# State-space mixer: state sums by accumulating transposes, and four units scanned wholly in PSUM

## The chip, the cores and the metric

The program runs on one core of a Trainium2 chip. The metric is the device time of one execution in microseconds (us), the median of several runs. The engines are TensorE (PE, with its weight loads PEld), VectorE (DVE), ScalarE (ACT), GpSimd (POOL) and SyncE (SP), which here issues all the transfers.

## The reference

A feed-forward block, a mixer and the same feed-forward block again work on x of 4 sequences of 2048 tokens and 512 channels, all in f32. The change is in the mixer alone:

```
xz = x_in @ W_in;  x, z = split(xz)            # 1024 channels each
x  = silu(depthwise_conv4(x) + conv_b)
Bm, Cm = split(x @ W_x)                         # 16 states each
delta  = softplus(x @ W_dt + b_dt)
# for each channel d and state s, over tokens t:
h[d,s] = exp(delta[t,d] * A[d,s]) * h[d,s] + delta[t,d] * Bm[t,s] * x[t,d]
y[t,d] = sum_s h[d,s] * Cm[t,s]
out = ((y + x * D) * silu(z)) @ W_out + residual
```

## The kernel before, in words

The mixer cuts the 8192 tokens into 32 chunks of 256 tokens (the columns of a tile) and the 1024 channels into 8 blocks b of 128 (the partitions). The 16 states of a block are taken as 4 groups g of 4. One **unit** n = 4b+g is one group of one block, so that a chunk is 32 units, and a unit has two **pairs** of states (`half` 0 and 1).

For each unit:

- GpSimd makes `dbu` = delta·x·B for two units at once (`times_b`, L948), into a ring of 4 units.
- ScalarE makes exp(delta·A) of two states into one of three PSUM banks `ps_da` (L1154). First it waits until that bank is free. If the bank held a first pair, it must first copy the last column of the states aside (`keep_psum`, L1095), and for that VectorE's product with C (L1257) must be done.
- VectorE runs four scans (L1245). The first pair is scanned in its PSUM bank; the second pair from PSUM into the SBUF ring `hp`.
- The first pair is multiplied by C on VectorE into `hc` (`times_c`, L1257), the second pair by GpSimd in place in `hp` (L961), for two units at once where it can (in the last block one at a time).
- TensorE adds the products: a matmul with the identity as the stationary operand and 256 columns moving, into the PSUM bank `ps_y` of the block (two banks, taken in turn): L1395 for `hc`, L1405 for `hp`. 20 of a chunk's 64 states in `hp` are not added there but by VectorE (`add_state`, L1224): three in each odd block and two in each even one.
- When a block's sum is complete, VectorE multiplies it by the gate (`gated`, L1231). The skip term x·D was written into `ps_y` beforehand by ScalarE (`skip`, L1016), before the first sum of the block.

Beside this run, for later units or the next chunk: the input product (L1333) and its convolution (ScalarE L1003, then three steps on VectorE, L1211), the gate product (L1344) and its copy (L1023), the delta product (L1362) with ScalarE's abs, relu, exp and log (L1062 to L1071), the product for B and C (L1353), and the output product (L1372). Four times a chunk ScalarE loads the table for silu, runs silu on z and on u, and loads the exp table again (L1183, L1028, L1009, L1188). I call this **the table block**; it stands after the exps of a unit n with n mod 8 = 5.

The order of work is written out by hand. A list such as `YG_AT` gives for each block the unit in whose step an engine does the thing; `due` looks it up, also for the neighbouring chunks. All engines walk through the same 32 steps, and semaphores hold them together.

Of the kernel before, what the change touches and what calls it, by code (L numbers as in the profile page):

```python
# [687 lines left out]
def mixer_phase(nc, hT_pad, xs_in, ahead, w_dt, w_out, w_k, mu_r, mu_k, bc_dram, out):  # L688
# [8 lines left out]
    with ExitStack() as ctx:  # L697
# [297 lines left out]
        def _(act):  # L995
# [143 lines left out]
            def body(i, par, first):  # L1139
                for n in range(NU):  # L1140
# [3 lines left out]
                    for half in range(2):  # L1144
                        p = 2 * n + half
                        if before(p) % 2:
                            bank_scanned(i, p)
                        else:
                            keep_psum(i, p)
                        if before(p) % 2 == 0:  # L1150
                            psum_kept(i, p)
# [46 lines left out]
        def _(dve):  # L1198
# [15 lines left out]
            def added_before(c, b):  # L1214
                return sum(len(a) for a in ADDED) * c + sum(len(a) for a in ADDED[:b])

            def add_state(c, b, k):

                y = y_sum(b)
                if k == 0:  # L1220
                    dve.wait_ge(s_r, NU * c + NG * (b + 1))
                else:
                    dve.wait_ge(s_ya, added_before(c, b) + k)
                V.tensor_tensor(y, y, hp[:, ADDED[b][k] % NH, SG - SD - 1, :], ALU.add).then_inc(s_ya, 1)  # L1224
# [323 lines left out]
```

## Time and profile before

| | us |
|---|---|
| median of 3 runs | 5237.82 (5236.78 to 5240.89) |
| span of the profiled execution | 5236.4 |
| PE busy in the span | 5093.7 (97%) |
| DVE | 4729.5 (90%) |
| POOL | 4028.2 (77%) |
| ACT | 3830.1 (73%) |

The time of the profiled execution is its span; what the runs show beyond it is 1.4 us at the median. The mixer fills the span from about 665 us to 4630 us; before and behind it are the two feed-forward blocks. The busy shares over the whole span mix the three. Two neighbouring instructions of one engine overlap a little in the rows, so what an instruction costs its engine is read from its start to the start of the next, which is less than its duration.

### The profile page before, as it was taken

To read this page: it belongs to the slowest core of one execution; us is meant where nothing else is said; L and a number is where in the kernel's file an instruction comes from. 1 tells how busy PE (TensorE), PEld (TensorE's weight loads), DVE (VectorE), ACT (ScalarE), POOL (GpSimd) and SP (SyncE) were. 2 spreads that over 40 slices of the span, in tenths; PEclk is the share of its full clock that TensorE was granted. 3 is DMA by queue.
4 is the path that set the end of the run, shared out by engine and by line. 5 is a ranking of instruction groups with operands and counts; after the bars stand their busy time and mean duration, and the time that the engine had idled before them with its cause. 6 is when DMAs were issued, how large, how long until landed. Compare 5 with 4: busy or idle time off the path is not lost. (4 is left out here: it accounts for less than half of the span.)

```text
span 5236.4 us, 76648 instructions
## 1 busy us (share of the span) xinstructions
PE 5093.7 (97%) x22144; PEld 4077.0 (78%) x22144; DVE 4729.5 (90%) x8180; ACT 3830.1 (73%) x9592; POOL 4028.2 (77%) x1701
## 2 busy tenths in 40 slices
PE   8999989999999999999999999999999999989999
PEld 6777767777777777777777777777777777768887
DVE  6777679999999999999999999999999999977775
ACT  5566468888888888888888888888888888744443
POOL 1111069999999999999999999999999999931110
PEclk9999999999999999999999999999999999989999
DMA  2222231111111111111111111111111111111111
GB/s 83 96 73 83 99 109 45 45 45 53 57 53 49 45 45 45 45 45 45 50 52 48 46 52 55 53 54 45 45 45 45 45 45 45 65 53 57 65 57 41
DMA packets 137370, 291.71 MB, mean 56 GB/s; under 512 B 23280, under 2 KB 40688, under 8 KB 136944
## 3 DMA queue, kind: packets, MB, share of 16 engines
q1 hardware_dynamic: 136944, 286.75, 16.5%
q8 instruction: 180, 2.95, 0.2%
q14 instruction: 246, 2.02, 0.1%
HBM read 218.53 MB, written 68.18 MB: 55 GB/s over the span
## 5 line engine op out<-in xcount | busy, mean ns | idle before, releaser
L948 POOL TENSOR_TENSOR mx_dbu<-mx_bs,mx_du 128x2048 f32<-128x2048 f32 (+1 forms) x513 | 2326.9, 4536 | 60.0 <-DVE mx_hp L1245 49.8
L1154 ACT ACTIVATE mx_ps_da<-mx_dl,mx_a 128x256 f32<-128x256 f32 x4096 | 1775.8, 465 | 53.8 <-DVE mx_hp L1245 19.0
L1245 DVE TENSOR_TENSOR_SCAN mx_hp<-mx_ps_da,mx_hst,mx_dbu 128x256 f32<-128x256 f32 x1792 | 1313.9, 733 | 30.9 <-ACT mx_ps_da L1154 30.9
L1245 DVE TENSOR_TENSOR_SCAN mx_ps_da<-mx_ps_da,mx_hst,mx_dbu 128x256 f32<-128x256 f32 x1792 | 1248.8, 736 | 21.6 <-ACT mx_ps_da L1154 15.7
L961 POOL TENSOR_TENSOR mx_hp<-mx_hp,mx_cs 128x1024 f32<-128x1024 f32 (+1 forms) x576 | 1224.7, 2133 | 1.7 <-ACT mx_hst L1077 1.7
L1395 PE MATMUL mx_ps_y<-mx_hc,mx_ident 128*128 128x256 f32 x4096 | 1054.7, 380 | 2.0 <-ACT mx_ps_y L1016 2.0
L1362 PE MATMUL mx_ps_m<-mx_u,mx_w_dt 128*128 128x256 f32 x4096 | 927.7, 380 | 2.3 <-issue 2.3
L1395 PEld LDWEIGHTS mx_ps_y<-mx_hc,mx_ident 128*128 128x128 f32 x4096 | 779.9, 190 | 109.8 <-ACT mx_ps_y L1016 2.8
L1362 PEld LDWEIGHTS mx_ps_m<-mx_u,mx_w_dt 128*128 128x128 f32 x4096 | 779.2, 190 | 109.4 <-issue 3.1
L1405 PE MATMUL mx_ps_y<-mx_hp,mx_ident 128*128 128x256 f32 x2816 | 787.3, 383 | 50.6 <-POOL mx_hp L961 50.5
L1405 PEld LDWEIGHTS mx_ps_y<-mx_hp,mx_ident 128*128 128x128 f32 x2816 | 525.6, 190 | 233.3 <-issue 87.9
L1257 DVE TENSOR_TENSOR mx_hc<-mx_ps_da,mx_cs 128x512 f32<-128x512 f32 x1024 | 682.1, 666 | 4.1 <-issue 2.1
L1095 ACT ACTIVATE mx_hst<-mx_ps_da 128x2 f32<-128x2 f32 x1022 | 171.2, 168 | 632.6 <-DVE mx_hc L1257 631.6
L246 POOL TENSOR_TENSOR f_rstd<-f_ve,f_half 128x4 f32<-128x4 f32 x48 | 48.4, 1009 | 681.3 <-DVE f_ve L413 681.3
L1344 PE MATMUL mx_ps_m<-mx_hT,mx_w_in 128*128 128x256 f32 x2048 | 493.8, 383 | 24.8 <-DVE mx_u L1211 23.8
L1333 PE MATMUL mx_ps_m<-mx_hT,mx_w_in 128*128 128x259 f32 x2048 | 492.2, 383 | 5.1 <-PEq L59 3.2
L1333 PEld LDWEIGHTS mx_ps_m<-mx_hT,mx_w_in 128*128 128x128 f32 x2048 | 389.4, 190 | 104.7 <-issue 46.4
L1372 PE MATMUL mx_ps_c<-mx_w_out,mx_gy 128*128 128x512 f32 x992 | 467.2, 593 | 0.0
L1344 PEld LDWEIGHTS mx_ps_m<-mx_hT,mx_w_in 128*128 128x128 f32 x2048 | 381.0, 190 | 108.0 <-DVE mx_u L1211 56.0
L1211 DVE SCALAR_TENSOR_TENSOR mx_u<-mx_ps_m,mx_cw,mx_u 128x256 f32<-128x256 f32 x768 | 354.9, 462 | 28.6 <-ACT mx_u L1003 27.8
L252 POOL TENSOR_TENSOR mx_w_in<-f_xhT 128x2048 f32<-128x2048 f32 x30 | 112.1, 3738 | 324.2 <-ACT f_xhT L302 324.2
L1372 PEld LDWEIGHTS mx_ps_c<-mx_w_out,mx_gy 128*128 128x128 f32 x992 | 189.1, 191 | 132.1 <-issue 119.2
(122 smaller groups left out, 7378.5 us busy)
## 6 DMA issues: line engine op xcount, KB each, us to landing
mx_bs<-bc_scratch SPq DMA_DIRECT2D x128, 512.0 KB, 4.6
mx_cs<-bc_scratch SPq DMA_DIRECT2D x128, 512.0 KB, 3.8
mx_hT<-hT_scratch SPq DMA_DIRECT2D x32, 518.0 KB, 4.2
hT_scratch<-f_h2T SPq DMA_DIRECT2D x16, 1024.0 KB, 9.1
mx_xo<-xs_scratch SPq DMA_DIRECT2D x32, 512.0 KB, 3.6
x_scratch<-mx_xo SPq DMA_DIRECT2D x32, 512.0 KB, 2.9
f_x<-in_L_attn_inp SPq DMA_DIRECT2D x12, 1024.0 KB, 6.6
xs_scratch<-f_x SPq DMA_DIRECT2D x12, 1024.0 KB, 4.3
```

The lines of the kernel that those rows point to most:

```text
L948: G.tensor_tensor(dbu[:, n % NM:n % NM + k].rearrange("p n s t -> p (n s) t"), bs[:, g:g + k].rearrange("p n s t -> p (n s) t"), bcast(du[ ...
L961: G.tensor_tensor(h, h, cs[:, g:g + k, SD:SG, :], ALU.mult).then_inc(s_pr, k)
L1154: ins = A.activation(ps_da[DA_BANK[p]][:, k, :], dl[:, b % NL, :], ACT.Exp, scale=a_sb[:, b, s:s + 1])
L1211: V.scalar_tensor_tensor(out=q, in0=in_bank(b)[:, step:step + T], scalar=cw[:, step, b:b + 1], in1=q, op0=ALU.mult, op1=ALU.add).then_inc( ...
L1245: ins = V.tensor_tensor_scan(da if half == 0 else hp[:, n % NH, k, :], da, dbu[:, n % NM, s, :], 0.0 if first else hst[:, b, SG * g + s:SG ...
L1257: V.tensor_tensor(hc[:, n % NC, :, :], ps_da[DA_BANK[2 * n]][:, :, :], cs[:, g, 0:SD, :], ALU.mult).then_inc(s_m2, 1)
L1333: ins = M.matmul(in_bank(b)[:, 0:TH], w_in_sb[:, f, b * P:(b + 1) * P], hT[cp][:, f, :], start=(f == 0), stop=(f == NB - 1))
L1344: ins = M.matmul(m_bank(b)[:, 0:T], w_in_sb[:, f, DI + b * P:DI + (b + 1) * P], hT[cp][:, f, PAD_L:PAD_L + T], start=(f == 0), stop=(f == ...
L1362: ins = M.matmul(m_bank(b)[:, 0:T], w_dt_sb[:, k, b * P:(b + 1) * P], u[:, cp, k, :], start=(k == 0), stop=(k == ND - 1))
L1372: ins = M.matmul(ps_c[:, :], gy[:, cp, b, j * P:(j + 1) * P], w_out_sb[:, b, :], start=False, stop=(b == ND - 1), skip_group_check=True)
L1395: ins = M.matmul(y_sum(b), ident[:, :], hc[:, n % NC, k, :], start=False, stop=False, skip_group_check=True)
L1405: ins = M.matmul(y_sum(b), ident[:, :], hp[:, n % NH, k, :], start=False, stop=(g == NG - 1), skip_group_check=True)
```

## The change

- **The sum.** The matmul with the identity is gone. Each product with C is now turned: the data is the stationary operand, the identity moves, and the transpose accumulates in `ps_y` (`turn_onto`). `ps_y` holds tokens in the partitions and channels in the columns. A state of 256 tokens takes two transposes of 128 columns. All states are summed so; `add_state` on VectorE is gone, with its 20 instructions a chunk.
- **Back.** When a block is complete, ScalarE copies it to the new tile `yt` (`copy_y`), then writes the skip term into `ps_y` (`skip`, which stood at step 4b+3, ahead of the block's first sum, and now stands at step 4b+9, behind its last), and TensorE turns `yt` back onto it with two transposes (`turn_back`). The gate product on VectorE (`gated`) moves from step 4b+9 to step 4b+10.
- **Units 4, 5, 20 and 21.** Their second pair is scanned in PSUM too, and VectorE multiplies it by C into the new tile `hx` (`times_c_second`), one unit later, behind the next unit's first scan. GpSimd's product for these units (two instructions a chunk) is gone. ScalarE keeps the state of these pairs from PSUM (`keep_psum` for them too).

```diff
-        SKIP_AT = [NG * b + NG - 1 for b in range(ND)]
-        ADDED = [[n for n in range(NG * b + 1 + (b % 2 == 0), NG * (b + 1))] for b in range(ND)]
-        YG_AT = [NG * b + NG + 5 for b in range(ND)]
+        YT_AT = [NG * b + NG + 5 for b in range(ND)]
+        BACK_AT = [NG * b + NG + 5 for b in range(ND)]
+        YG_AT = [NG * b + NG + 6 for b in range(ND)]
+        ALL_IN_PSUM = (4, 5, 20, 21)
...
+            def copy_y(c, b):
+                act.wait_ge(s_r, NU * c + NG * (b + 1))
+                A.activation(yt[:, b % 2, :], y_sum(b), ACT.Copy).then_inc(s_yt, 1)
+
             def skip(c, cp, b):
                 act.wait_ge(s_u, ND * c + 2 * (b // 2) + 2)
-                if not (is0(c) and b < 2):
-                    act.wait_ge(s_g, ND * c + (b - 1))
+                act.wait_ge(s_yt, ND * c + (b + 1))
                 A.activation(y_sum(b), u[:, cp, b, :], ACT.Copy, scale=d_sb[:, b:b + 1]).then_inc(s_yd, 1)
...
                     scan(i, n, 0, 0, first)
-                    add_due(i, n, 0)
+                    if n - 1 in ALL_IN_PSUM:
+                        times_c_second(i, n - 1)
                     scan(i, n, 0, 1, first)
-                    add_due(i, n, 1)
...
+            def times_c_second(i, n):
+                g, e = n % NG, extra(n)
+                dve.wait_ge(s_sc, 2 * NU * i + (2 * n + 2))
+                if not (is0(i) and e < NX2):
+                    dve.wait_ge(s_rcx, NE * i + (e - NX2 + 1))
+                V.tensor_tensor(hx[:, e % NX2, :, :], ps_da[DA_BANK[2 * n + 1]][:, :, :], cs[:, g, SD:SG, :],
+                                ALU.mult).then_inc(s_m2x, 1)
...
+            def turn_onto(b, pair, first):
+                for k in range(SD):
+                    for j in range(TJ):
+                        ins = M.matmul(y_sum(b)[:, j * P:(j + 1) * P], pair[:, k, j * P:(j + 1) * P], ident[:, :],
+                                       is_transpose=True, start=(first and k == 0 and j == 0), stop=False,
+                                       skip_group_check=True)
+                return ins
...
             def sum_psum_states(c, n):
                 b, g = divmod(n, NG)
-                if g == 0:
-                    pe.wait_ge(s_yd, ND * c + (b + 1))
+                if g == 0 and not (is0(c) and b < 2):
+                    pe.wait_ge(s_g, ND * c + (b - 1))
                 pe.wait_ge(s_m2, NU * c + (n + 1))
-                for k in range(SD):
-                    ins = M.matmul(y_sum(b), ident[:, :], hc[:, n % NC, k, :],
-                                   start=False, stop=False, skip_group_check=True)
-                ins.then_inc(s_rc, 1)
+                turn_onto(b, hc[:, n % NC], g == 0).then_inc(s_rc, 1)
...
+            def turn_back(c, b):
+                pe.wait_ge(s_yd, ND * c + (b + 1))
+                for j in range(TJ):
+                    ins = M.matmul(y_sum(b)[:, j * P:(j + 1) * P], yt[:, b % 2, j * P:(j + 1) * P], ident[:, :],
+                                   is_transpose=True, start=False, stop=(j == TJ - 1), skip_group_check=True)
+                ins.then_inc(s_yb, 1)
```

The program also asks for a smaller scratch for transfers that GpSimd would issue (`dynamic_dma_scratch_size=1024`); no transfer in either kernel is issued by GpSimd.

**VectorE in a table block's steps, before.** These are the rows of steps 5 and 6 (mod 8) of a chunk's middle, from the last convolution step of step 4. L1245 is a scan (into `ps_da` for the first pair, into `hp` for the second), L1257 the product with C, L1224 an added state, L1231 the gate.

```order
L1211 SCALAR_TENSOR_TENSOR mx_u<-mx_ps_m,mx_cw,mx_u 128x256
L1245 SCALAR_TENSOR_TENSOR mx_ps_da<-mx_ps_da,mx_hst,mx_dbu 128x256
L1224 TENSOR_TENSOR mx_ps_y<-mx_ps_y,mx_hp 128x256
L1245 SCALAR_TENSOR_TENSOR mx_ps_da<-mx_ps_da,mx_hst,mx_dbu 128x256
L1224 TENSOR_TENSOR mx_ps_y<-mx_ps_y,mx_hp 128x256
L1245 SCALAR_TENSOR_TENSOR mx_hp<-mx_ps_da,mx_hst,mx_dbu 128x256
L1257 TENSOR_TENSOR mx_hc<-mx_ps_da,mx_cs 128x512
L1224 TENSOR_TENSOR mx_ps_y<-mx_ps_y,mx_hp 128x256
L1245 SCALAR_TENSOR_TENSOR mx_hp<-mx_ps_da,mx_hst,mx_dbu 128x256
L1231 TENSOR_TENSOR mx_gy<-mx_ps_y,mx_gy 128x256
```

The same steps in the changed kernel, where lines 1253, 1275, 1288 and 1261 stand for 1211, 1245, 1257 and 1231:

```order
L1253 SCALAR_TENSOR_TENSOR mx_u<-mx_ps_m,mx_cw,mx_u 128x256
L1275 SCALAR_TENSOR_TENSOR mx_ps_da<-mx_ps_da,mx_hst,mx_dbu 128x256 x2
L1275 SCALAR_TENSOR_TENSOR mx_hp<-mx_ps_da,mx_hst,mx_dbu 128x256
L1288 TENSOR_TENSOR mx_hc<-mx_ps_da,mx_cs 128x512
L1275 SCALAR_TENSOR_TENSOR mx_hp<-mx_ps_da,mx_hst,mx_dbu 128x256
L1275 SCALAR_TENSOR_TENSOR mx_ps_da<-mx_ps_da,mx_hst,mx_dbu 128x256 x2
L1275 SCALAR_TENSOR_TENSOR mx_hp<-mx_ps_da,mx_hst,mx_dbu 128x256
L1288 TENSOR_TENSOR mx_hc<-mx_ps_da,mx_cs 128x512
L1275 SCALAR_TENSOR_TENSOR mx_hp<-mx_ps_da,mx_hst,mx_dbu 128x256
L1261 TENSOR_TENSOR mx_gy<-mx_ps_y,mx_gy 128x256
```

The three added states are gone from step 5, and the gate stands one step later, at the end of step 6.

**ScalarE around a table block, before.** L1095 and L1077 keep states, L1154 are the exps of a pair, L1183 and L1188 the two table loads with silu of z and u between, L1062 and L1063 abs and relu, L1023 the gate product's copy, L1067 the exp of the softplus, L1016 the skip term.

```order
L1077 ACTIVATE mx_hst<-mx_hp 128x2
L1154 ACTIVATE mx_ps_da<-mx_dl,mx_a 128x256 x2
L1095 ACTIVATE mx_hst<-mx_ps_da 128x2
L1154 ACTIVATE mx_ps_da<-mx_dl,mx_a 128x256 x2
L1077 ACTIVATE mx_hst<-mx_hp 128x2
L1183 ACT_TABLE_LOAD
L1028 ACTIVATE mx_gy<-mx_gy 128x512
L1009 ACTIVATE mx_u<-mx_u 128x512
L1188 ACT_TABLE_LOAD
L1154 ACTIVATE mx_ps_da<-mx_dl,mx_a 128x256 x2
L1062 ACTIVATE mx_en<-mx_ps_m,mx_bdt 128x256
```

The same in the changed kernel (1116, 1192, 1136, 1222, 1065, 1042, 1227 and 1099 stand for 1077, 1154, 1095, 1183, 1028, 1009, 1188 and 1062; L1047 is `copy_y`, L1053 `skip`):

```order
L1116 ACTIVATE mx_hst<-mx_hp 128x2
L1192 ACTIVATE mx_ps_da<-mx_dl,mx_a 128x256 x2
L1047 ACTIVATE mx_yt<-mx_ps_y 128x256
L1053 ACTIVATE mx_ps_y<-mx_u,mx_d 128x256
L1136 ACTIVATE mx_hst<-mx_ps_da 128x2
L1192 ACTIVATE mx_ps_da<-mx_dl,mx_a 128x256 x2
L1116 ACTIVATE mx_hst<-mx_hp 128x2
L1222 ACT_TABLE_LOAD
L1065 ACTIVATE mx_gy<-mx_gy 128x512
L1042 ACTIVATE mx_u<-mx_u 128x512
L1227 ACT_TABLE_LOAD
L1192 ACTIVATE mx_ps_da<-mx_dl,mx_a 128x256 x2
```

The copy and the skip term now stand just before the exps that lead into the table block; from that block on the order is as it was.

**TensorE from a delta product over a gate product, before** (L1362 the delta product, L1344 the gate product, L1353 the product for B and C):

```order
L1362 MATMUL mx_ps_m<-mx_u,mx_w_dt 128x256 x8
L1405 MATMUL mx_ps_y<-mx_hp,mx_ident 128x256 x2
L1395 MATMUL mx_ps_y<-mx_hc,mx_ident 128x256 x2
L1344 MATMUL mx_ps_m<-mx_hT,mx_w_in 128x256 x4
L1405 MATMUL mx_ps_y<-mx_hp,mx_ident 128x256 x2
L1395 MATMUL mx_ps_y<-mx_hc,mx_ident 128x256 x2
L1353 MATMUL mx_ps_c<-mx_u,mx_w_x 32x256 x8
```

and in the changed kernel (1395, 1377 and 1386 stand for 1362, 1344 and 1353; L1425 is `turn_onto`, L1453 `turn_back`):

```order
L1395 MATMUL mx_ps_m<-mx_u,mx_w_dt 128x256 x8
L1425 MATMUL mx_ps_y<-mx_ident,mx_hp 128x128 x4
L1425 MATMUL mx_ps_y<-mx_ident,mx_hc 128x128 x4
L1377 MATMUL mx_ps_m<-mx_hT,mx_w_in 128x256 x4
L1425 MATMUL mx_ps_y<-mx_ident,mx_hp 128x128 x4
L1425 MATMUL mx_ps_y<-mx_ident,mx_hc 128x128 x4
L1453 MATMUL mx_ps_y<-mx_ident,mx_yt 128x128 x2
L1386 MATMUL mx_ps_c<-mx_u,mx_w_x 32x256 x8
```

Two or one wide matmuls become four narrow transposes, and two more stand behind the gate product's step.

## Rows read from the trace of the kernel before

**Rows 1.** Windows; stretch, length, busy (count) PE PEld DVE ACT POOL, clock, DMA.

```profile
2000.00:3000.00 1000.00, 987.15 (x4248) 790.68 (x4247) 978.41 (x1730) 815.36 (x2206) 983.24 (x408) 1.00 0.15 49
...
4480.00:4600.00 120.00, 107.59 (x423) 81.81 (x422) 113.53 (x191) 91.32 (x253) 120.00 (x51) 0.96 0.19 62
```

**Rows 2.** Instructions of one tile, 1880:2045; count, ns, first to last start.

```profile
L1055 ACT ACTIVATE mx_bc<-mx_ps_c x2: 357/357/357, 1900.8 to 2023.1; 32x256 f32<-32x256 f32 x2
```

**Rows 3.** Timeline, VectorE, a table block's steps; start, duration, engine, line.

```profile
2017.33 0.75 DVE L1245 TENSOR_TENSOR_SCAN mx_hp<-mx_ps_da,mx_hst,mx_dbu 128x256 f32<-128x256 f32 x1 [0.33 <-ACT mx_ps_da L1154]
...
2039.53 0.67 DVE L1257 TENSOR_TENSOR mx_hc<-mx_ps_da,mx_cs 128x512 f32<-128x512 f32 x1
...
2042.21 0.40 DVE L1224 TENSOR_TENSOR mx_ps_y<-mx_ps_y,mx_hp 128x256 f32<-128x256 f32 x1
2042.52 0.74 DVE L1245 TENSOR_TENSOR_SCAN mx_ps_da<-mx_ps_da,mx_hst,mx_dbu 128x256 f32<-128x256 f32 x1
...
2045.72 0.39 DVE L1231 TENSOR_TENSOR mx_gy<-mx_ps_y,mx_gy 128x256 f32<-128x256 f32 x1
2046.17 1.40 DVE L1245 TENSOR_TENSOR_SCAN mx_ps_da<-mx_ps_da,mx_hst,mx_dbu 128x256 f32<-128x256 f32 x2
2047.90 0.75 DVE L1245 TENSOR_TENSOR_SCAN mx_hp<-mx_ps_da,mx_hst,mx_dbu 128x256 f32<-128x256 f32 x1 [0.33 <-ACT mx_ps_da L1154]
```

**Rows 4.** Timeline, ScalarE, the same table block.

```profile
2040.24 0.17 ACT L1095 ACTIVATE mx_hst<-mx_ps_da 128x2 f32<-128x2 f32 x1 [1.59 <-DVE mx_hc L1257]
...
2045.27 0.87 ACT L1154 ACTIVATE mx_ps_da<-mx_dl,mx_a 128x256 f32<-128x256 f32 x2
...
2046.99 0.87 ACT L1154 ACTIVATE mx_ps_da<-mx_dl,mx_a 128x256 f32<-128x256 f32 x2
...
2047.90 0.36 ACT L1023 ACTIVATE mx_gy<-mx_ps_m 128x256 f32<-128x256 f32 x1
...
2049.27 0.46 ACT L1016 ACTIVATE mx_ps_y<-mx_u,mx_d 128x256 f32<-128x256 f32 x1
...
2055.98 0.17 ACT L1095 ACTIVATE mx_hst<-mx_ps_da 128x2 f32<-128x2 f32 x1 [0.93 <-DVE mx_hc L1257]
```

**Rows 5.** Timeline, TensorE, identity sums between delta and gate product.

```profile
2040.36 1.03 PE L1405 MATMUL mx_ps_y<-mx_hp,mx_ident 128*128 128x256 f32 x4
2041.22 1.03 PE L1395 MATMUL mx_ps_y<-mx_hc,mx_ident 128*128 128x256 f32 x4
2042.08 1.89 PE L1344 MATMUL mx_ps_m<-mx_hT,mx_w_in 128*128 128x256 f32 x8
```

**Rows 6.** Timeline, TensorE, eight transposes in the first feed-forward block.

```profile
321.48 1.09 PE L566 MATMUL f_ps_t<-f_ident,f_h 128*128 128x128 f32 x8
322.32 0.48 PE L601 MATMUL f_ps_kr<-f_w_lo,f_xr_hi 128*128 128x512 f32 x1
322.64 0.41 PE L602 MATMUL f_ps_kr<-f_w_hi,f_xr_hi 128*128 128x512 f32 x1
```

**Rows 7.** Timeline, GpSimd: its product with C for two units.

```profile
2035.26 2.37 POOL L961 TENSOR_TENSOR mx_hp<-mx_hp,mx_cs 128x1024 f32<-128x1024 f32 x1
```

**Rows 8.** Windows as rows 1: around the fall of TensorE's clock near 2668 us.

```profile
2664.71:2668.12 3.41, 1.29 (x6) 1.17 (x7) 1.88 (x4) 2.34 (x8) 3.41 (x4) 1.00 0.40 133
2668.12:2671.54 3.42, 3.42 (x10) 2.67 (x9) 3.42 (x8) 2.34 (x9) 3.42 (x1) 0.50 0.61 180
```

**Rows 9.** Timeline, TensorE: delta products in and outside that stretch.

```profile
2036.90 3.62 PE L1362 MATMUL mx_ps_m<-mx_u,mx_w_dt 128*128 128x256 f32 x16
...
2666.82 5.40 PE L1362 MATMUL mx_ps_m<-mx_u,mx_w_dt 128*128 128x256 f32 x16 [2.32 <-issue]
```

**Rows 10.** Windows, the transposes (tile f_ps_t) alone: PE busy, clock, DMA.

```profile
4641.03:4644.44 3.41, 3.41 (x17) 0.50 0.96 350
4644.44:4647.86 3.42, 1.06 (x8) 1.00 0.00 1
```

More of the change, by code:

```diff
@@ L41 @@
 NC = 4
+NX2 = 2
 NH = 8
@@ L799, in mixer_phase, with in_psum, extra, step_to @@
         DA_BANK = [p % NA for p in range(2 * NU - 1)] + [1]
+        ALL_IN_PSUM = (4, 5, 20, 21)
+        NE = len(ALL_IN_PSUM)
+        def in_psum(p):
+            return p % 2 == 0 or p % (2 * NU) // 2 in ALL_IN_PSUM
+        def extra(n):
+            return sum(m < n for m in ALL_IN_PSUM)
+        def step_to(n):
+            k = 1
+            while n - k in ALL_IN_PSUM:
+                k += 1
+            return k
+        def last_in_sbuf(n):
+            while n % NU in ALL_IN_PSUM:
+                n -= 1
+            return n
         def is0(i):
@@ L1145, in body @@
                         p = 2 * n + half
-                        if before(p) % 2:
+                        if in_psum(before(p)):
+                            keep_psum(i, p)
+                        else:
                             bank_scanned(i, p)
[L1148 to L1151, printed above, removed]
                         for k in range(SD):
@@ L1160, in body @@
                                 first_tap(i + s, (par + s) % 2, bb)
-                            for bb, s in due(SKIP_AT, n, i):
+                            for bb, s in due(YT_AT, n, i):
+                                copy_y(i + s, bb)
                                 skip(i + s, (par + s) % 2, bb)
@@ L1193, in epilogue @@
                         keep(LAST, NU + n - KEEP_LAG)
+                    for b in due_after(YT_AT, n):
+                        copy_y(LAST, b)
+                        skip(LAST, LAST % 2, b)
             over_chunks(act, prologue, body, epilogue)
@@ L1212, in conv @@
                                        in1=q, op0=ALU.mult, op1=ALU.add).then_inc(s_cq if step == KC - 1 else s_cv, 1)
[L1214 to L1224, printed above, removed]
             def gated(c, cp, b):
@@ L1309, in epilogue @@
                     for b in due_after(YG_AT, n):
-                        for k in range(len(ADDED[b])):
-                            add_state(LAST, b, k)
                         gated(LAST, LAST % 2, b)
@@ L1453, in body @@
                         sum_psum_states(i - 1, NU + n - SUMC_LAG)
+                    for b, s in due(BACK_AT, n, i):
+                        turn_back(i + s, b)
             def epilogue():
-                for n in range(SUM_LAG):
+                for n in range(BACK_AT[-1] + 1 - NU):
+                    if n < SUM_LAG:
+                        sum_states(LAST, NU + n - SUM_LAG)
+                    if n < SUMC_LAG:
+                        sum_psum_states(LAST, NU + n - SUMC_LAG)
+                    for b in due_after(BACK_AT, n):
+                        turn_back(LAST, b)
                     if n == 2:
```

73 lines of the change are left out of this document (41 added, 32 removed).

## The prediction

> **What bounds the kernel now.** I read the busy time in windows first. In the mixer's steady part three engines look full at once: TensorE 987, GpSimd 983 and VectorE 978 us of 1000; ScalarE has 815 [rows 1]. A share alone doesn't say which of the three sets the pace, so I looked for a chain that closes on itself. One chunk lasts 122.3 us (the copy of B and C, once a chunk, starts at 1900.8 and 2023.1) [rows 2], and a chunk has four table blocks, so eight steps last 30.6 us.
>
> The timeline of VectorE around a table block shows the chain. I cut the eight steps at two places: the product with C of step 4 (mod 8) and the third scan of step 6.
>
> - Stretch A, from the product at 2039.53 to the scan at 2047.90, is 8.37 us [rows 3]. ScalarE runs it. The product ends, ScalarE keeps the state at 2040.24, makes two exps, loads the table, runs silu twice, loads the table back, makes the exps at 2045.27, abs and relu, and the exps at 2046.99; the scan starts 0.04 us after these end [rows 4]. VectorE waits twice in it: two scans that start at 2046.17 would have let the third start 1.30 us later (1.40 less the usual overlap of 0.1), at 2047.47, so 0.43 are lost there, and about 0.14 between the gate at 2045.72 (0.31 long, start to start) and 2046.17. VectorE's own work in A is thus 7.8 us.
> - Stretch B, from such a scan at 2017.33 to the product at 2039.53, is 22.20 us [rows 3], VectorE without a gap.
>
> A and B give 30.57, four times 122.3: the chunk exactly. TensorE and GpSimd are nearly full, but the chain that closes is VectorE and ScalarE. That is the reading on which the forecast rests: **what VectorE saves in B counts, what it saves in A becomes a longer wait for ScalarE.**
>
> **VectorE.** An added state costs 0.31 (2042.21 to 2042.52) [rows 3], 0.32 as a mean. Of the 20 of a chunk, 12 (three in each odd block) stand in step 5, in A, and 8 (two in each even block) in step 1, in B. The gates leave steps 1 and 5 and come to steps 2 and 6, both in B. So B loses two states and a gate and gains two gates: 22.20 − 0.64 + 0.31 = 21.87. A's own work falls by three states and a gate, 1.27, to 6.5, far below 8.37: A stays as it is and the wait grows from 0.6 to 1.8 us.
>
> The second product of units 4, 5, 20 and 21 costs 0.67 less the overlap of 0.09, 0.58 [rows 3]. For both pairs of units it stands in A (steps 5 and 6), where there is room. Only its order shows: the exps at 2045.27 are ready at 2046.14, 6.6 us into A, and then a scan (0.65), the product (0.58) and a scan (0.65) come before the third scan, 8.52 instead of 8.37. A scan into PSUM costs what one into SBUF does, since both are 0.65 apart in B's steps.
>
> **ScalarE.** It gains a copy of 256 columns from PSUM in each block, 0.36 as the gate product's [rows 4], and a semaphore wait on itself before the skip term of 0.46; together some 0.8 us in step 1 (mod 4), between its two exps. There it waits now for the product with C: 1.59 us before the table block [rows 4], 0.93 in the tightest such step that I found [rows 4]. So it is hidden, with 0.1 us to spare there. The skip term leaves step 3, where ScalarE was just catching up behind the table block. Keeping the second pairs from PSUM (0.17) replaces keeping them from SBUF in the four units. Bounds of this edit: nothing, and the whole 0.8 us in each of 8 steps, 6.4 us a chunk, if no wait covered it.
>
> **TensorE.** A chunk has 64 + 44 = 108 identity matmuls. Four records, two matmuls, take 0.86 (2040.36, 2041.22, 2042.08) [rows 5], so 46.4 us go. 256 transposes and 16 turned back come. Eight take 0.84 (321.48 to 322.32) and the first matmul after them is 0.32 from the next where 0.23 is usual [rows 6], so 0.105 each and some 0.14 for each of the 32 groups of eight: 28.6 + 4.5 = 33.1 us. TensorE falls from 120.7 us a chunk (98.7%) [rows 1] to about 107. These transposes write and don't add; one that accumulates isn't shown. From above I bound it by the transposes at the lower clock, 17 in 3.41 us, 0.20 each [rows 10]; that would be +26 us, 133 in all. TensorE would set the pace from 0.155 each on. I take 0.105, the row that is nearest: same shape, same clock.
>
> What queues behind the new waits: TensorE's `turn_back` in step 4b+9 waits for ScalarE's skip term of the same step. In front of it stand the gate product (from 2042.08, 1.73 long) and eight transposes, while ScalarE's exps of that step ended before 2040.24; so it is there in time. The first sum of block b+2 in step 4b+11 now waits for VectorE's gate at the end of step 4b+10; behind it stand the delta products, needed only by relu two steps later. TensorE will idle some 1 us there and 2.5 us before the gate product, whose convolution ends only with step 0 (mod 4). That is idle time of an engine with 14 us a chunk to spare.
>
> **GpSimd.** Two products with C of 2.37 [rows 7] leave each chunk: 4.7 us of about 120. It isn't in the chain, except in the last chunk, where no input products are left and GpSimd is busy 120.00 of 120.00 us from 4480 to 4600 [rows 1]. There I count 3.5 us. The end of the mixer: three added states become copy, skip term and two transposes, about 1.3 us each way, nothing.
>
> **The sum.** Per chunk four times (−0.64 + 0.31), and twice +0.15: −1.0 us. 31 chunks: −31; the last: −3.5. Together −34.5 on the profiled execution's 5236.4, so 5202. The runs' median is 1.4 above that execution: 5203.
>
> At the clock I weigh a rule. Transposes alone filled the stretch from 4641.03 to 4644.44 at the granted clock 0.50, and it was 1.00 in the next [rows 10]: TensorE did nothing but transposes and rose to 2.4 GHz. The Trainium skill, TensorE: Matmul & The Clock Gate, Part 4 (PE-mode transpose), says that in transpose mode the full clock doesn't engage, because a transpose isn't counted as activity. By this rule a quarter of TensorE's work would turn into apparent idleness and the mixer could sink to 1.2 GHz; here the trace disagrees.
>
> **The rivals.**
>
> 1. *All of VectorE's saving arrives* (the table block isn't the limit). 20 × 0.32 − 4 × 0.58 = 4.1 us a chunk, 5237.8 − 131 = 5107. For it: GpSimd (about 115.5 us then) and TensorE (107) would allow it, and 815 of 1000 us leaves ScalarE room on average. Against: the scan at 2047.90 starts 0.04 us after its exps, with the added states still in A.
> 2. *TensorE's clock falls in its new idle stretches* (slower). Between 2664.71 and 2668.12 TensorE was busy 1.29 of 3.41 us, and the next 3.4 us ran at 0.50 [rows 8]; the delta product at 2666.82 took 5.40 us where 3.62 is usual [rows 9], 1.8 us lost. My idle stretch of 2.5 us before a gate product is as long as the 2.32 there. Eight falls a chunk add 14 us: 121.4 against a chunk of 121.3. It decides where four steps are full already. They hold 107 / 8 = 13.4 us of 15.2 on average, and some 1.3 more in two of the eight: where the product for B and C stands (eight matmuls, about 3.5 as the delta product, and no output product) and where two output products do. A fall makes each of these 14.7 + 1.8 = 16.5, late by 1.3, and a chunk lasts 121.3 + 2.6 = 123.9: +1.5 a chunk, 5237.8 + 48 = 5286. For it: the idle stretches are real. Against: a late TensorE waits less before the next gate product, so falls thin themselves out.
> 3. *ScalarE's 0.8 us doesn't fit* in step 1 (mod 4): if the wait between copy and skip term costs 0.25 more than I think, 0.12 us in each of eight steps eat the gain: 5237.
> 4. *The clock sinks throughout* by the rule above: TensorE twice 107 us a chunk, +92 × 32: 8170.
>
> **How the numbers follow.** A change within 0.2%, 10.5 us, can't be told from none here. Forecast 0.53, its own range 5190 to 5222, all faster. Rival 1 0.12, faster. Rival 2 0.19, slower but for mild cases. Rival 3 0.13, split over no change and its two sides. Rival 4 0.03. Faster 0.64, same 0.14, slower 0.22. For the range I leave out rivals 1 and 4 and half a tenth beyond rival 2: 5140 to 5290; the low end takes in the part of rival 1 in which A shortens somewhat.
>
> **What would show it.** In the profile after: the distance of two copies of B and C 121.3 us; the third scan of step 6 waiting for ScalarE's exps by 1.3 to 1.8 us four times a chunk, in all some 1.6 × 4 × 32 = 200 us of VectorE's idle time before its scans, released by ScalarE's exps; the table block itself unchanged; transposes 0.105 us apart; TensorE's busy share near 90%, GpSimd's near 95%. The forecast is wrong if A is shorter than 8.3 us, if the delta or input products wait for anything but their old partners, if TensorE's clock in the mixer's windows is below 0.97 and ScalarE waits for its products, or if VectorE shows no new wait.

## The result, and the profile after

The changed kernel takes 5295.2 us (median of 4 runs, 5294.0 to 5296.5), the kernel before 5239.4: 1.0108 times as long, 95% interval 1.0093 to 1.0122. The forecast was 5203. It had the wrong sign, and the time lies 5 us above its range of 5140 to 5290.

In the profiled executions (5236.4 and 5292.2) the copy of B and C cuts the span into its start, 31 chunks and the end. Tile view of that copy, before and then after; count, ns, first to last start:

```profile
L1055 ACT ACTIVATE mx_bc<-mx_ps_c x32: 357/357/373, 692.1 to 4471.8; 32x256 f32<-32x256 f32 x32
```

```profile
L1092 ACT ACTIVATE mx_bc<-mx_ps_c x32: 357/357/374, 692.0 to 4532.7; 32x256 f32<-32x256 f32 x32
```

The start is the same. The 31 chunks take 3779.7 before and 3840.7 after, +61.0; the rest 764.6 and 759.5, −5.1. Together, but for 0.1 at the start, +55.8: all of the loss lies in the chunks. They take 123.9 us on average, 121.9 before; the forecast's cut of 1.0 would have made it 120.9. The averages hold the first chunk and those at a change of sequence (every eighth), which are shorter. A chunk in a sequence's middle takes 122.5 or 122.6 before and 124.1 to 125.8 after. Windows of after (columns as rows 1); the second begins and ends with a copy of B and C, the last three lie around the loss:

```profile
2000.00:3000.00 1000.00, 879.51 (x4629) 701.94 (x4628) 926.92 (x1572) 828.06 (x2232) 930.13 (x387) 0.96 0.15 48
...
1916.00:2041.20 125.20, 110.84 (x577) 88.49 (x576) 116.46 (x197) 103.03 (x279) 115.78 (x49) 0.95 0.15 47
...
1967.97:1971.38 3.41, 1.09 (x8) 0.86 (x8) 2.63 (x6) 3.35 (x11) 3.41 (x2) 1.00 0.00 0
1971.38:1974.79 3.41, 1.78 (x2) 0.84 (x3) 3.41 (x7) 2.88 (x9) 2.24 (x2) 0.51 0.01 2
1974.79:1978.21 3.42, 3.42 (x7) 2.01 (x6) 2.64 (x5) 0.00 (x0) 1.93 (x1) 0.50 0.00 0
```

Against [rows 1] no engine is full any more, and the granted clock is 0.96 and not 1.00. The longest waits of after between 1000 and 4500 us (total, times, longest) say who waits. The first and the last weren't in the forecast:

```profile
ACT mx_u L1036 <- PE mx_ps_m L1366: 166.0, 59, 5.6
DVE mx_ps_da L1275 <- ACT mx_ps_da L1192: 138.3, 114, 1.7
...
DVE mx_hp L1275 <- ACT mx_ps_da L1192: 106.0, 85, 4.0
...
PE mx_ps_c L1405 <- DVE mx_gy L1261: 86.7, 28, 3.5
```

28 times in 28 chunks an output product waits for a gate. The timelines of one such chunk (1916.00 to 2041.20) show what hangs on it. TensorE first:

```profile
1968.96 0.60 PE L1425 MATMUL mx_ps_y<-mx_ident,mx_hc 128*128 128x128 f32 x4
1973.01 3.78 PE L1405 MATMUL mx_ps_c<-mx_w_out,mx_gy 128*128 128x512 f32 x4 [3.45 <-DVE mx_gy L1261]
1976.59 2.74 PE L1366 MATMUL mx_ps_m<-mx_hT,mx_w_in 128*128 128x259 f32 x8
```

ScalarE, the exps before its wait and the first tap after it:

```profile
1973.44 0.86 ACT L1192 ACTIVATE mx_ps_da<-mx_dl,mx_a 128x256 f32<-128x256 f32 x2
1979.36 0.56 ACT L1036 ACTIVATE mx_u<-mx_ps_m,mx_cb,mx_cw 128x256 f32<-128x256 f32 x1 [5.07 <-PE mx_ps_m L1366]
```

VectorE over the whole chunk: the products with C of step 4 (L1288), the third scans of step 6, and the gate and the stall between:

```profile
1931.85 0.68 DVE L1288 TENSOR_TENSOR mx_hc<-mx_ps_da,mx_cs 128x512 f32<-128x512 f32 x1
...
1938.50 1.40 DVE L1275 TENSOR_TENSOR_SCAN mx_ps_da<-mx_ps_da,mx_hst,mx_dbu 128x256 f32<-128x256 f32 x2 [1.37 <-ACT mx_ps_da L1192]
1940.22 0.75 DVE L1275 TENSOR_TENSOR_SCAN mx_hp<-mx_ps_da,mx_hst,mx_dbu 128x256 f32<-128x256 f32 x1 [0.33 <-ACT mx_ps_da L1192]
...
1962.09 0.68 DVE L1288 TENSOR_TENSOR mx_hc<-mx_ps_da,mx_cs 128x512 f32<-128x512 f32 x1
...
1970.68 0.72 DVE L1275 TENSOR_TENSOR_SCAN mx_hp<-mx_ps_da,mx_hst,mx_dbu 128x256 f32<-128x256 f32 x1
...
1972.56 0.39 DVE L1261 TENSOR_TENSOR mx_gy<-mx_ps_y,mx_gy 128x256 f32<-128x256 f32 x1
...
1980.93 0.75 DVE L1275 TENSOR_TENSOR_SCAN mx_hp<-mx_ps_da,mx_hst,mx_dbu 128x256 f32<-128x256 f32 x1 [3.50 <-ACT mx_ps_da L1192]
...
1996.13 0.68 DVE L1288 TENSOR_TENSOR mx_hc<-mx_ps_da,mx_cs 128x512 f32<-128x512 f32 x1
...
2004.51 0.75 DVE L1275 TENSOR_TENSOR_SCAN mx_hp<-mx_ps_da,mx_hst,mx_dbu 128x256 f32<-128x256 f32 x1 [0.33 <-ACT mx_ps_da L1192]
...
2026.38 0.68 DVE L1288 TENSOR_TENSOR mx_hc<-mx_ps_da,mx_cs 128x512 f32<-128x512 f32 x1
...
2035.26 0.72 DVE L1275 TENSOR_TENSOR_SCAN mx_hp<-mx_ps_da,mx_hst,mx_dbu 128x256 f32<-128x256 f32 x1
```

Read in order: the output product of blocks 6 and 7 stands in step 7 of the next chunk and needs the gate of block 7, which the change moved from the end of step 5 to the end of step 6. TensorE had its sums done near 1969.5; the gate ends at 1972.95. Meanwhile the clock goes to the lower of its levels (0.51, 0.50: 1.2 GHz), so the output product takes 3.78 us and not 1.88, and the input product behind it 2.74 and not 1.92. The first tap waits 5.07 us for it, and no exps are made meanwhile; VectorE's scan waits 3.50 us for those.

| stretch | before | forecast | after |
|---|---|---|---|
| A, no extra unit | 8.37 | 8.37 | 8.37, 8.38 |
| A of units 4 and 5, scanned in PSUM after | 8.37 | 8.52 | 8.59 |
| A of units 20 and 21, scanned in PSUM after | 8.64 | 8.52 | 8.88 |
| B | 22.20 | 21.87 | 21.87, 21.87 |
| B with step 7 | 22.20 | 21.87 | 25.45 |

The stretches B without step 7 and A without extra units came out as forecast, and A with them is 0.07 and 0.36 longer. The stretch with step 7 has 3.58 us too much: 3.50 of it is that one wait.

The stretch A of units 20 and 21 was already 8.64 in the kernel before, which the forecast had missed. It runs there from the product below to the scan at 2017.33 [rows 3], and ScalarE has one instruction more in it, ahead of the table block (L1048, which clears the bank for B and C):

```profile
2008.69 0.68 DVE L1257 TENSOR_TENSOR mx_hc<-mx_ps_da,mx_cs 128x512 f32<-128x512 f32 x1
```

```profile
2010.56 0.36 ACT L1048 ACTIVATE mx_ps_c<-mx_w_x 32x256 f32<-32x256 f32 x1
```

So the extra units lengthen either stretch A by the same amount, 0.22 and 0.24, where 0.15 was forecast.

### The profile page after: what moved, and what is told of

The parts are those of the page before. It is cut to its first block and busy times, and to the rows that moved or that the text cites. A ratio compares the mean times of both kernels' runs of the same rounds, so it can differ in the third digit from the quotient of the medians.

```text
span 5292.2 us, 79790 instructions
## 1 busy us (share of the span) xinstructions
PE 4723.0 (89%) x23936; PEld 3774.3 (71%) x23936; DVE 4592.8 (87%) x7668; ACT 3937.5 (74%) x9848; POOL 3879.9 (73%) x1637
## 5 line engine op out<-in xcount | busy, mean ns | idle before, releaser
L1275 DVE TENSOR_TENSOR_SCAN mx_ps_da<-mx_ps_da,mx_hst,mx_dbu 128x256 f32<-128x256 f32 x2016 | 1404.8, 736 | 134.7 <-ACT mx_ps_da L1192 133.1
L1275 DVE TENSOR_TENSOR_SCAN mx_hp<-mx_ps_da,mx_hst,mx_dbu 128x256 f32<-128x256 f32 x1568 | 1145.6, 731 | 101.1 <-ACT mx_ps_da L1192 101.1
L994 POOL TENSOR_TENSOR mx_hp<-mx_hp,mx_cs 128x1024 f32<-128x1024 f32 (+1 forms) x512 | 1070.9, 2099 | 1.7 <-ACT mx_hst L1116 1.7
L1377 PE MATMUL mx_ps_m<-mx_hT,mx_w_in 128*128 128x256 f32 x2048 | 541.9, 410 | 309.0 <-DVE mx_u L1253 309.0
L1288 DVE TENSOR_TENSOR mx_hc<-mx_ps_da,mx_cs 128x512 f32<-128x512 f32 x1024 | 681.9, 666 | 2.3 <-PE mx_ps_y L1425 2.2
L1425 PE MATMUL mx_ps_y<-mx_ident,mx_hc 128*128 128x128 f32 x4096 | 629.6, 277 | 22.8 <-DVE mx_gy L1261 22.7
L1425 PEld LDWEIGHTS mx_ps_y<-mx_ident,mx_hp 128*128 128x128 f32 x3584 | 447.1, 143 | 259.4 <-POOL mx_hp L994 116.9
L1425 PE MATMUL mx_ps_y<-mx_ident,mx_hp 128*128 128x128 f32 x3584 | 552.6, 278 | 79.6 <-POOL mx_hp L994 79.4
L1405 PE MATMUL mx_ps_c<-mx_w_out,mx_gy 128*128 128x512 f32 x992 | 523.6, 654 | 93.4 <-DVE mx_gy L1261 93.4
L1366 PE MATMUL mx_ps_m<-mx_hT,mx_w_in 128*128 128x259 f32 x2048 | 511.1, 393 | 5.3 <-PEq L60 3.2
L1425 PEld LDWEIGHTS mx_ps_y<-mx_ident,mx_hc 128*128 128x128 f32 x4096 | 490.3, 144 | 30.7 <-DVE mx_gy L1261 16.2
L1366 PEld LDWEIGHTS mx_ps_m<-mx_hT,mx_w_in 128*128 128x128 f32 x2048 | 394.8, 199 | 116.4 <-issue 61.0
```

The source lines that it names most:

```text
L1275: ins = V.tensor_tensor_scan(da if in_psum(p) else hp[:, n % NH, k, :], da, dbu[:, n % NM, s, :], 0.0 if first else hst[:, b, SG * g + s:S ...
L1288: V.tensor_tensor(hc[:, n % NC, :, :], ps_da[DA_BANK[2 * n]][:, :, :], cs[:, g, 0:SD, :], ALU.mult).then_inc(s_m2, 1)
L1366: ins = M.matmul(in_bank(b)[:, 0:TH], w_in_sb[:, f, b * P:(b + 1) * P], hT[cp][:, f, :], start=(f == 0), stop=(f == NB - 1))
L1377: ins = M.matmul(m_bank(b)[:, 0:T], w_in_sb[:, f, DI + b * P:DI + (b + 1) * P], hT[cp][:, f, PAD_L:PAD_L + T], start=(f == 0), stop=(f == ...
L1405: ins = M.matmul(ps_c[:, :], gy[:, cp, b, j * P:(j + 1) * P], w_out_sb[:, b, :], start=False, stop=(b == ND - 1), skip_group_check=True)
L1425: ins = M.matmul(y_sum(b)[:, j * P:(j + 1) * P], pair[:, k, j * P:(j + 1) * P], ident[:, :], is_transpose=True, start=(first and k == 0 an ...
```

## The experiments

Theory 1: the chunk loses its 3 us in step 7, by the output product's wait for gate 7 and the clock's fall in it. Rivals: the clock's falls at the other new idle places (forecast's rival 2), or ScalarE's new copy and skip term.

**The wait removed from either end, and the idle time filled.** Three kernels from the changed one:

```diff
-OUT_AT = [NU - 6, NU - 2, NU + 2, NU + 7, ...
+OUT_AT = [NU - 6, NU - 2, NU + 2, NU + 8, ...
```

> The changed kernel, with the one output product that waits for the gate of block 7 issued in TensorE's step 8 of the next chunk, not in step 7, so that the input product of step 7 no longer stands behind that wait. Theory (the missed wait): after the change this output product waits 3.45 us for the gate that was moved from step 37 to step 38, TensorE's clock falls meanwhile, and the input product, ScalarE's first tap (5.07 us) and VectorE's scan (3.50 us in some 20 chunks, 2.3 in the others) come late one after the other. Then the chunk loses these waits: 5295 - 20x3.5... less what other waits take over, 5220 (5210 to 5232). Rival (the clock falls at all the new idle places and costs there): the other falls stay, less than half comes back, 5260 or more. Rival (ScalarE's copy and skip, and its block of table loads): nothing of theirs is touched, 5290 or more.

```diff
-YG_AT = [NG * b + NG + 6 for b in range(ND)]
+YG_AT = [NG * b + NG + (5 if b == ND - 1 else 6) for b in range(ND)]
```

> The changed kernel, with VectorE's gate of block 7 alone back at the end of step 37 of 32 (step 5 of the next chunk), where it stood before; the other seven gates stay a step later. The output product keeps its place in step 7. Theory (the missed wait): same gain by the other end of the same wait, 5220 (5210 to 5232), if the turn back is done by then (it ended at 1967.3 in the changed trace, VectorE's step 5 at 1970.0). Rival (clock falls everywhere): 5260 or more. Rival (ScalarE's work): 5290 or more. If gate 7 has to wait for the turn back, VectorE waits instead and the time lies between.

```diff
 j, k = divmod(part, OUT_PARTS)
+if part == 3:
+    for b, s2 in due(IN_AT, n, i):
+        pe.wait_ge(s_rl, ND * (i + s2 - 1) + b)
+        for m in range(2 * NB):
+            M.matmul(in_bank(b)[:, 0:TH], ...)
```

> The changed kernel, with TensorE kept busy in the once-per-chunk wait: ahead of the output product in step 7, 16 products of the input product's shape (3.5 us at full clock) into the bank that the input product then overwrites. The wait for gate 7 stays; only the idle time goes, and with it the fall of the clock. Theory that the clock carries most of the loss: the output product takes 1.9 us and not 3.8, the input product 1.8 and not 2.7, the first tap comes 2.8 us earlier, VectorE's 3.5 us wait shrinks to 0.7: 5225 to 5240. Theory that the wait for the gate alone carries it: 5285 to 5300, or more, since the filler also ends some tenths after the gate.

Measured against the kernel before (5238.4; 5239.8 and 5239.7 beside the later runs): output product later 5198.5, 0.9924 (0.9907 to 0.9940); gate 7 back 5188.0, 0.9904 (0.9887 to 0.9920); filler 5236.6, 0.9997 (0.9988 to 1.0007). Removing the wait gives back 97 and 107 us, more than the 75 expected; both times lie below the expected 5210 to 5232. I had counted the full stall of VectorE in 20 chunks only and added little for the others. In the trace of the changed kernel VectorE waits at this place in each of 30 chunks, 2.3 to 4.0 us, in all 96.2 us, nearly the whole of the 96.7. The wait is the longer the more of the output and the input product falls into the stretch at the lower clock. Windows of the kernel with gate 7 back, two whole chunks:

```profile
2126.40:2247.70 121.30, 108.29 (x578) 87.15 (x577) 116.37 (x197) 103.15 (x279) 115.78 (x49) 0.97 0.15 49
...
3216.40:3337.70 121.30, 105.45 (x577) 84.78 (x577) 116.37 (x197) 103.24 (x280) 115.83 (x49) 1.00 0.15 49
```

Both last 121.3 us, one at a mean clock of 0.97 and one at 1.00. So the falls that are left (most of them in the idle time before gate products) cost nothing here, and that rival falls. The other rival, ScalarE's copy and skip term, falls too: nothing of theirs was touched, and the loss is gone.

The filler keeps the wait for the gate and takes the idle time. Its TensorE, L1489 the filler, and then its VectorE:

```profile
1956.71 3.78 PE L1489 MATMUL mx_ps_m<-mx_hT,mx_w_in 128*128 128x259 f32 x16
1960.33 1.88 PE L1405 MATMUL mx_ps_c<-mx_w_out,mx_gy 128*128 128x512 f32 x4
1962.04 1.92 PE L1366 MATMUL mx_ps_m<-mx_hT,mx_w_in 128*128 128x259 f32 x8
```

```profile
1959.73 0.40 DVE L1261 TENSOR_TENSOR mx_gy<-mx_ps_y,mx_gy 128x256 f32<-128x256 f32 x1
...
1965.56 0.75 DVE L1275 TENSOR_TENSOR_SCAN mx_hp<-mx_ps_da,mx_hst,mx_dbu 128x256 f32<-128x256 f32 x1 [0.97 <-ACT mx_ps_da L1192]
```

With 16 products more, whose results are thrown away, the kernel is 58.6 us faster than the changed one: the output product takes 1.88 again, and VectorE's wait falls from 3.50 to 0.97. Against the kernel with the output product later (the same gates), the loss of 96.7 us splits into 58.6 for the clock and 38.1 for the rest. The 38.1 holds the late gate itself and some 4 us of the filler's own, an estimate (30 chunks of 0.14): the output product starts 0.20 us after the gate's end here (1960.13 to 1960.33), and 0.06 in the changed kernel (1972.95 to 1973.01). The clock's share is thus 58.6 us or a little more.

**All gates back in step 4b+9,** and then also the gate product moved to the end of TensorE's step, behind the sums and the turn back:

```diff
-YG_AT = [NG * b + NG + 6 for b in range(ND)]
+YG_AT = [NG * b + NG + 5 for b in range(ND)]
```

> The changed kernel, with all eight gates at the end of VectorE's step 4b+9, as before the change. Theory (the missed wait): as for gate 7 alone, 5220, and the 0.78 us waits of the first PSUM sums for a gate go too, which stand beside other work and give nothing: within 6 us of the kernel that moves gate 7 alone. Rival: the turn back of a block comes after a gate product that itself waits for VectorE (2.44 us idle, then 1.9 to 3.0 us of products), so VectorE waits for it at the end of step 4b+9: 0.3 to 1 us in 7 of 8 blocks, 70 to 250 us in all, and the kernel is at or over 5290.

```diff
-for b, s in due(GATE_AT, n, i):
-    gate_product(i + s, (par + s) % 2, b)
 ...
 for b, s in due(BACK_AT, n, i):
     turn_back(i + s, b)
+for b, s in due(GATE_AT, n, i):
+    gate_product(i + s, (par + s) % 2, b)
```

> All eight gates at the end of VectorE's step 4b+9, as in the kernel of 5238.0, and in TensorE's steps 1 mod 4 the gate product is issued behind the sums and the turn back, not ahead of them. Theory (the extra 50 us of that kernel were VectorE's wait for a turn back that stood behind a waiting gate product): that wait goes, every second gate now lies in VectorE's idle time before step 6 mod 8 (4 x 0.31 us a chunk), and it beats the kernel with gate 7 alone put back: 5150 to 5185. Rival (the 50 us came from having the gates in step 4b+9 at all, or the gate product now comes too late behind the sums): 5200 or more.

All gates back: 5238.0, 0.9998 (0.9988 to 1.0007), 50 us worse than gate 7 alone, where within 6 us was expected. The rival named the right wait, but too large: it had 70 to 250 us and a time of 5290 or more. TensorE and VectorE at one such gate:

```profile
2054.62 3.53 PE L1377 MATMUL mx_ps_m<-mx_hT,mx_w_in 128*128 128x256 f32 x8 [3.11 <-DVE mx_u L1253]
...
2059.01 0.38 PE L1453 MATMUL mx_ps_y<-mx_ident,mx_yt 128*128 128x128 f32 x2
```

```profile
2059.50 0.42 DVE L1261 TENSOR_TENSOR mx_gy<-mx_ps_y,mx_gy 128x256 f32<-128x256 f32 x1 [1.75 <-PE mx_ps_y L1453]
```

The gate product waits 3.11 us and then runs at half speed (3.53, not 1.9); the turn back stands behind it, and VectorE waits 1.75 us for that, 60.7 us in 3500 (46 waits). Here, and not in the changed kernel, a slow gate product reaches VectorE.

With the gate product last: 5163.2, 0.9855 (0.9839 to 0.9872), the fastest kernel that computes everything, 76 us under the kernel before and 132 under the changed one. Its chunks in the middle of a sequence take 120.3 us. The two orders also test the forecast's cut into A and B. With the output product later, all eight gates lie in B: 121.7 us. With gate 7 back, seven: 121.3. With the gate product last, four: 120.3. So 0.4 for the first gate that goes into A, and 1.0 for three more; a gate costs 0.31 by the prediction's reading.

**What stretch A waits for.** From the kernel with gate 7 back: ScalarE's block without its table loads, and Silu of u and z a plain copy (this leaves part of the computation out):

```diff
-A.preload_act_table_set("silu_and_others")
-A.preload_act_table_set("natural_log_exp_and_others")
-A.activation(q, q, ACT.Silu)
+A.activation(q, q, ACT.Copy)
```

> The kernel with gate 7 alone put back, and ScalarE's block of two table loads made short: it leaves out the table loads, and Silu of u and of z is a plain copy. Theory (stretch A is set by that block): VectorE's 5.3 us of waits a chunk for ScalarE's exponentials go, and VectorE (116.0) and GpSimd (115.8) are left as bounds: chunk 117 to 118.5, 5188 - 31 x 2.8 to 4.3 = 5055 to 5100. Rival (those waits are another chain's, GpSimd's or TensorE's, seen last at ScalarE): 5170 or more.

5060.1, 0.9654 (0.9638 to 0.9670), as expected. Windows:

```profile
2000.00:3000.00 1000.00, 914.11 (x4919) 734.43 (x4918) 983.01 (x1674) 794.09 (x2306) 987.50 (x410) 0.98 0.15 49
```

VectorE (983) and GpSimd (988) fill up at once, and most chunks last 116.2 to 117.6 us. Stretch A without extra units falls from 8.37 to 6.49 us (2039.41 to 2045.90 in this trace), which is VectorE's own work in it: the prediction had 6.5. The block is what stretch A waits for.

Then, from the fastest kernel, the block half a step later (it goes from the end of the step before):

```diff
+block = due(Z_SILU_AT, n, i, 1)
+if half == 0 and block:
+    ...            # table load, silu_z, silu_u, table load
+if half == (1 if block else 0):
     ...            # relu, as before
```

> The fastest kernel so far (5163.2; gates in step 4b+9, gate product last), with ScalarE's block of table load, Silu of z, Silu of u and table load moved by half a step: from the end of step 5 mod 8 to behind the first pair's exponentials of step 6 mod 8; the Abs and Relu of that step follow the second pair's exponentials. Theory (stretch A lasts from the product that frees a PSUM bank to the third scan, with the block ahead of both pairs' exponentials): the first pair of step 6 no longer waits for the block, VectorE's waits there fall from 1.05 + 0.33 to some 0.6: 0.5 to 1 us in each of four stretches, 5163 - 31 x 2 to 4 = 5040 to 5100. Rival (the bank of the first pair is free no earlier, so ScalarE waits for it ahead of the block and all shifts back): 5150 to 5180. Rival (the Silu of u comes later, and x_proj, its DMAs or the later Relu set the time): 5180 or more.

5217.0, 0.9956 (0.9939 to 0.9972): 54 us slower, a miss. ScalarE ahead of the block, and VectorE behind it:

```profile
2980.57 0.17 ACT L1140 ACTIVATE mx_hst<-mx_ps_da 128x2 f32<-128x2 f32 x1 [1.29 <-DVE mx_hx L1299]
...
2981.67 1.28 ACT L1196 ACT_TABLE_LOAD   x1
```

```profile
2986.53 0.75 DVE L1277 TENSOR_TENSOR_SCAN mx_hp<-mx_ps_da,mx_hst,mx_dbu 128x256 f32<-128x256 f32 x1 [1.22 <-ACT mx_ps_da L1192]
```

In the stretches with extra units the bank of step 6's first pair holds unit 4's second pair and is free only after its product with C: ScalarE waits 1.29 us for it ahead of the block, and these stretches A grow from 8.60 and 8.89 to 9.36. That is the first rival's wait, for these. In the other two stretches the gain is there, 7.63 for 8.38. Over a chunk the four stretches A are thus no longer than before; what is lost is lost in B. In the chunk from 2064.4 its four stretches take 22.10, 21.84, 22.49 and 21.84, where 21.51 to 21.53 was the rule, and in each of them VectorE waits once or twice more for exps, by 0.20 to 0.42 us. What holds these exps up there, the record leaves open.

**What the units in PSUM are worth.** None of them, from the kernel with gate 7 back (`ALL_IN_PSUM = ()`); eight, and two, from the fastest kernel (`(4, 5, 12, 13, 20, 21, 28, 29)` and `(4, 5)`):

> The kernel with gate 7 alone put back (5188.0), and no unit whose second pair is scanned in PSUM: the turned sums are all that is left of the change. VectorE loses four products a chunk (4 x 0.6 us), GpSimd gets four back (4 x 1.28 us: 115.8 busy in a chunk of 121.3 becomes some 121). Theory that VectorE and ScalarE's table blocks set the chunk: VectorE had waited for ScalarE where those four products stand, so their going gives nothing, and GpSimd just fits: 5185 to 5195. Rival that GpSimd sets it without them: 121.3 becomes 122.3 or more, 5215 to 5240.

> The kernel before this one in the list (gates in step 4b+9, gate product last), with four more units a chunk scanned in PSUM: 12, 13, 28, 29, the same steps of the blocks that had none. GpSimd loses 4 x 1.28 us a chunk, VectorE gains 4 x 0.6 us, two of them in each stretch where it waits 1.69 us for ScalarE's table block. Theory (VectorE and that block set the chunk): within 8 us of the kernel with four units. Rival (GpSimd's 95% busy still sets the pace outside that stretch): 20 to 60 us faster. Rival (PSUM banks come free later, so ScalarE's exponentials come later too, and the table block with them): 20 us slower or more.

> The same fastest kernel (5163.2) with two units a chunk scanned in PSUM (4 and 5) and not four. Theory (VectorE's work outside the wait for the table block sets the chunk, and GpSimd, 115.9 us busy in a chunk of 120.4 and now 118.4, still fits): 5155 to 5166. Rival (GpSimd's turns set it, and each pair of products that it is spared counts): 5175 to 5200. With four, two and none of the units (none: 5191.2, with the gates elsewhere) this tells what that half of the change is worth.

None: 5191.2, 0.9906 (0.9889 to 0.9923), beside 5188.0 with four. Windows:

```profile
2000.00:3000.00 1000.00, 881.35 (x4772) 706.79 (x4771) 937.22 (x1586) 850.89 (x2298) 994.05 (x413) 0.99 0.15 49
```

GpSimd is at 994 of 1000, just inside. The stretches A are 8.38 and, for units 20 and 21, 8.65, as in the kernel before, so their growth with four units is the units'. Two: 5166.9, 0.9861 (0.9844 to 0.9877), 4 us from four. Eight: 5209.0, 0.9942 (0.9925 to 0.9958), 46 us slower than four, where I expected no difference; chunks of 122.2 instead of 120.3. Two more stretches A grow from 8.38 to 8.60, 0.44 us a chunk. The rest lies in the stretch B that leads into the next chunk, 22.6 to 23.1 where the others take 21.5: there a new wait appears, once a chunk (VectorE's waits, 1000 to 4500 us):

```profile
DVE mx_hc L1288 <- DMA mx_cs<-bc_scratch: 20.2, 15, 1.8
DVE mx_hc L1288 <- issue: 17.2, 13, 2.4
```

15 of the 28 are put down to the transfer of the next chunk's C (`mx_cs`); for the other 13 the profile names no cause. Neither rival named it (the second, 20 us slower or more, is right in size alone), and why the transfer comes late is open. So four units, two or none make a difference of 3 to 4 us, under 0.1%, which can't be told from nothing here; the gain of the two fast kernels comes from the other half of the change, the transposes with the gates' places. In the middle of a sequence the kernel with no unit even has the shorter chunk, 120.9 for 121.3.

## Why the prediction was wrong

- **The step that failed** is "What queues behind the new waits". It followed the moved gate to one waiter, the first sum of block b+2, and said that behind it stand the delta products, with two steps to spare. It missed the second waiter, which thus stood in the sum at nothing: the output product of blocks 6 and 7, two steps after the old place of gate 7 and one after the new one, with the input product, the tap and the exps behind it. It costs 96.7 us (5295.2 to 5198.5 with that product a step later), 58.6 of them by the clock's fall. Without that wait the kernel takes 5198.5, or 5188.0 with gate 7 back in A; the forecast was 5203. That product waits for the gate by its last block's number, so it would have been found by listing every wait on the gates' semaphore. One of the prediction's own signs of being wrong came true: the clock below 0.97 while ScalarE waits for TensorE's products (166.0 us, first tap).
- **How good the rest was** is partly luck. "The chunk exactly" was chance: 122.3 is the distance of two copies early in a sequence, where the chunks in its middle take 122.5 or 122.6, since one stretch A in four is 8.64. From there the forecast's −1.0 would be 121.5 or 121.6, and the kernel with the output product later has 121.6 to 121.9. In the total that is more than made up by the three chunks at a change of sequence, which are 4.0 to 4.9 us shorter than before, and the first two, some 2 us each; the forecast had 1.0 for these too.
- **Stretch B, 21.87:** right to the hundredth. **Stretch A:** right where no unit was added; with units 0.07 and 0.36 over the forecast (8.59, 8.88), 0.27 of the larger because that stretch was 8.64 before. **VectorE's new waits** of 1.3 to 1.8 us for the exps are there in the stretches without extra units: 1.37 + 0.33.
- **ScalarE's copy and skip term** cost nothing: A without extra units and B came out at the 8.37 and 21.87 that were summed without them. That ended rival 3.
- **Transposes:** 0.44 us for four, 0.11 each, where 0.105 was taken. With gate 7 back TensorE has 105.5 us a chunk at full clock, 107 forecast. Timeline of after; at 2000.12 and 2000.56 four transposes that accumulate, and behind them the two that turn back:

```profile
2000.12 0.60 PE L1425 MATMUL mx_ps_y<-mx_ident,mx_hp 128*128 128x128 f32 x4
2000.56 0.60 PE L1425 MATMUL mx_ps_y<-mx_ident,mx_hc 128*128 128x128 f32 x4
2001.00 0.38 PE L1453 MATMUL mx_ps_y<-mx_ident,mx_yt 128*128 128x128 f32 x2
```

- **Rival 1** (all of VectorE's saving arrives) is out: VectorE's busy time in a chunk fell from some 120.5 to 116.4, and the chunk with gate 7 back is 121.3. The kernel without the table loads shows what it hides behind.
- **Rival 2** (the clock) named a mechanism that is part of the loss, at the wrong place; that its time, 5286, is near the measured one is chance. (Its 123.9 less 122.3 is 1.6 a chunk, not 1.5: some 3 us more.) It had the clock fall before gate products; those falls are there and were absorbed: the first product below runs at the fallen clock inside a stretch B of 21.87. The fall that counts lies in a wait I had not seen, and there it is 58.6 of the loss. The sentence "a late TensorE waits less before the next gate product" held: the second product below waits for nothing, and so do all 27 that come next after a gate product with a fallen clock, between 1000 and 4500 us.

```profile
1950.08 2.98 PE L1377 MATMUL mx_ps_m<-mx_hT,mx_w_in 128*128 128x256 f32 x8 [2.44 <-DVE mx_u L1253]
...
1964.25 2.00 PE L1377 MATMUL mx_ps_m<-mx_hT,mx_w_in 128*128 128x256 f32 x8
```

- **Rival 4** (the clock sinks throughout) is out: the clock was 0.96 in the steady part, and a chunk with all its 272 transposes ran at a mean of 1.00 (3216.40 to 3337.70 with gate 7 back). Against the rule of the Trainium skill, TensorE: Matmul & The Clock Gate, Part 4, that full clock doesn't engage in transpose mode, this says less than [rows 10], since two thirds of TensorE's busy time in that chunk are other products.
- **The last chunk and the end:** −5.1 where −3.5 was summed.

## What to carry to other kernels

When a step is moved later, list every wait on its semaphore, on every engine and across the turn of the loop, and ask for each what stands behind it in its queue; a wait on a count hides which item it is for. When TensorE waits once a chunk with work queued behind it, the fall of its clock can cost more than the wait: 58.6 against 38.1 us here. A fall of the clock in front of work that has slack cost nothing. Work of the bounding engine costs nothing only where that engine waits anyway: which side of the wait it stands on decides.

## What was not expected of the hardware

- Transposes that accumulate in PSUM cost what plain ones do: 0.11 us for 128x128 of float32, where plain ones took 0.105 [rows 6].
- A TensorE that was idle from 1969.56 to 1973.01 was granted 1.2 GHz (0.51 and 0.50) from 1971.38 to 1978.21, also while it was busy throughout (3.42 of 3.42 us). The same output product took 3.78 us there and 1.88 behind 3.6 us of products whose results are thrown away.
